# A long convolution with nine block products of a head in place of ten, and the summed index innermost

## The reference, cut to what matters

```python
vr = v.reshape(B, H, num_heads, L)                            # num_heads = 8; x1 and x2 are both the context
kv = vr[:, :, :, None, :] * x2r[:, :, None, :, :]             # b h i j l
y = irfft(rfft(kv, n=2 * L) * rfft(k, n=2 * L))[..., :L]      # causal convolution with the head's filter k[h]
y = y + kv * skip
out = jnp.einsum('bhijl,bhil->bhjl', y, x1r)                  # sum over i
```

## Time and profile before

| | |
|---|---|
| time, median of 3 runs | 2469.67 us (2468.76 to 2469.99) |
| profiled execution, its own time | 2451.03 us |
| span in its profile | 2448.9 us |
| PE busy in the span | 2185.6 us (89%) |
| DVE busy | 1212.2 us (49%) |
| ACT busy | 498.1 us (20%) |
| POOL busy | 437.4 us (18%) |

### The profile page before, as it was taken

The page is one execution under the profiler, slowest core; times in us unless marked ns, Lnnn a source line. Parts: engine busy times, 40 slices in busy tenths (PEclk is TensorE's granted clock), DMA queues, the critical chain, the costliest instruction groups (busy, mean ns, idle before and its releaser), DMA issues. The chain is left out here.

```text
span 2448.9 us, 30812 instructions
## 1 busy us (share of the span) xinstructions
PE 2185.6 (89%) x12383; PEld 1265.5 (52%) x12383; DVE 1212.2 (49%) x1811; ACT 498.1 (20%) x751; POOL 437.4 (18%) x445
## 2 busy tenths in 40 slices
PE   5888888867999989989999669899999999997964
PEld 3344444323444466645555346566665666664643
DVE  1456566655777752012222143445756666655354
ACT  1444444440000021111111011222222222121111
POOL 1111111113444413211111121101010110101000
PEclk9999999988999999999999879999999999998977
DMA  7000000004111047722211230101010110000000
GB/s 251 1 1 26 27 27 18 27 9 172 30 30 30 26 151 195 131 95 63 62 61 61 99 130 27 44 1 44 1 52 1 53 35 1 26 1 9 10 1 18
DMA packets 63856, 125.26 MB, mean 51 GB/s; under 512 B 12877, under 2 KB 13972, under 8 KB 63732
## 3 DMA queue, kind: packets, MB, share of 16 engines
q1 hardware_dynamic: 37492, 61.56, 7.6%
q10 hardware_dynamic: 19536, 43.26, 6.3%
q0 software_dynamic: 6704, 18.64, 2.7%
HBM read 92.18 MB, written 39.70 MB: 54 GB/s over the span
## 5 line engine op out<-in xcount | busy, mean ns | idle before, releaser
L863 PE MATMUL convB_conv<-kv,toep 128*128 128x512 f32 x640 | 277.8, 597 | 9.9 <-POOL kv L849 9.9
L1910 DVE RECIPROCAL tail_inv<-tail_ring 128x256 f32<-128x256 f32 x64 | 112.3, 1755 | 211.9 <-PE tail_ring L1566 211.9
L863 PEld LDWEIGHTS convB_conv<-kv,toep 128*128 128x128 f32 x640 | 122.6, 192 | 165.1 <-issue 156.6
L1294 PE MATMUL moe_gu_ps<-gu,moe_xT 128*128 x624 | 192.6, 462 | 2.2 <-DVE moe_xT L1357 2.2
L1294 PEld LDWEIGHTS moe_gu_ps<-gu,moe_xT 128*128 128x128 f32 x624 | 118.9, 191 | 79.3 <-issue 21.9
L849 POOL TENSOR_TENSOR kv<-vT,cT 128x512 f32 (+1 forms) x128 | 132.8, 1069 | 147.3 <-PE convB_conv L863 133.4
L888 DVE TENSOR_REDUCE vT<-prod 128x512 f32 (+1 forms) x128 | 138.2, 1080 | 16.7
L1741 POOL TENSOR_SCALAR_AFFINE_SELECT tail_expT<-tail_expT 128x1024 f32<-128x1024 f32 x64 | 70.9, 1107 | 368.8 <-ACT tail_expT L1803 368.7
L1312 PE MATMUL moe_y_ps<-down,moe_hT 128*128 (+1 forms) x234 | 110.7, 609 | 12.5 <-ACT moe_hT L1346 12.5
L1896 DVE TENSOR_TENSOR tail_allowed<-tail_scores,const_mask_bf 128x1024 f32<-128x1024 f32 x64 | 78.0, 1219 | 88.5 <-PE tail_scores L1518 87.9
L1735 POOL TENSOR_TENSOR tail_rstd_x<-tail_rstd_x,const_minus_half 128x2 f32<-128x2 f32 x32 | 22.3, 697 | 533.8 <-DVE tail_rstd_x L1868 533.8
(11 more groups left out here) (311 smaller groups left out, 3844.7 us busy)
## 6 DMA issues: line engine op xcount, KB each, us to landing
y_slots<-moe_y ACTq DMA_DIRECT2D x39, 256.0 KB, 2.0
toeplitz<-filt_pad SPq DMA_DIRECT2D x1, 8192.0 KB, 31.8
toep<-toeplitz SPq DMA_DIRECT2D x32, 256.0 KB, 2.6
gu<-in_L_ffn_gate_up_proj ACTq DMA_DIRECT2D x2, 2816.0 KB, 14.9
gu<-in_L_ffn_gate_up_proj SPq DMA_DIRECT2D x2, 2816.0 KB, 18.5
front_e<-in_ctx SPq DMA_DIRECT2D x8, 512.0 KB, 4.2
x_after<-x SPq DMA_DIRECT2D x8, 512.0 KB, 5.1
down<-in_L_ffn_down_proj ACTq DMA_DIRECT2D x2, 2048.0 KB, 18.3
```

The source lines that it names most:

```text
L863: ins = pe.matmul(conv[:, NC * p + lc, :], toep[p][:, lo:lo + P], kv[p][:, c].rearrange("p b i j -> p (b i j)"), start=c == 0, stop=c == lc)
L1294: ins = pe.matmul(gu_ps[:, s % 2, h, 0:HID], xT[:, c, :], wgu[c][:, e, h * HID:(h + 1) * HID], start=c == 0, stop=c == NC - 1)
L1910: link.after(dve.reciprocal(inv[c % 2][:], bank[:, S:2 * S]))
```

## The change

```diff
@@ front_stage, SP @@
                 load_x(0)
+                sp.dma_start(filt, filters).then_inc(filt_loaded, 16)
...
-                first_traffic(sp)
+                sp.wait_ge(steps_made, 2)
+                first_traffic(sp, filt, fall, rise)
...
+                        key = ("T", B - 2, len(T_UNITS) - 1)
+                        sp.wait_ge(quads.filled_sem(key), quads.count(key))
                         next_traffic(sp)
@@ front_stage, POOL @@
+                pool.wait_ge(filt_loaded, 16)
+                pool.tensor_tensor(fall, filt[:, 0:3 * P], filt[:, P:4 * P], ALU.subtract).then_inc(steps_made, 1)
+                pool.tensor_tensor(rise, filt[:, P:4 * P], filt[:, 0:3 * P], ALU.subtract).then_inc(steps_made, 1)
@@ front_stage, DVE @@
                 def combine(b, ab, t):
+                    if b + ab + t == 0:
+                        dve.wait_ge(pad_stored, 64)
@@ long_conv_stage @@
+        PARTS = {0: ((T0, 0),), 1: ((T1, 0), (T0, 1)), "both": ((T2, K01),), 2: ((T0, 2), (FALL, 1)),
+                 3: ((T1, 2), (RISE, 0), (T0, 3))}
+        KV_ORDER = (0, 1, K01, 2, 3)
...
+            @block.tensor
+            def _(pe):
+                for h in range(H):
+                    p = h % 2
+                    pe.wait_ge(mid.toep_loaded[p], 16 * (h // 2) + 16)
+                    for part in PARTS:
+                        last = max(KV_ORDER.index(c) for _, c in PARTS[part])
+                        pe.wait_ge(kv_ready, 5 * h + last + 1)
+                        bank = ring.claim(pe, (h, part))
+                        for n, (mat, c) in enumerate(PARTS[part]):
+                            ins = pe.matmul(bank, toep[p][:, mat * P:(mat + 1) * P], kv[p][:, c].rearrange("p b j i -> p (b j i)"),
+                                            start=n == 0, stop=n == len(PARTS[part]) - 1)
+                        ins.then_inc(ring.filled_sem((h, part)), 1)
...
+                for h in range(H):
+                    p = h % 2
+                    if h >= 2:
+                        pool.wait_ge(ring.filled_sem((h - 2, 3)), ring.count((h - 2, 3)))
+                    for n, c in enumerate(KV_ORDER):
+                        if c == K01:
+                            pool.wait_ge(kv_ready, 5 * h + n)
+                            pool.tensor_tensor(kv[p][:, K01], kv[p][:, 0], kv[p][:, 1], ALU.add).then_inc(kv_ready, 1)
+                        else:
+                            pool.tensor_tensor(kv[p][:, c], tokens_of(c, h), context_of(c, h, 3), ALU.mult).then_inc(kv_ready, 1)
...
+                for h in range(H):
+                    key = (h, "both")
+                    act.wait_ge(ring.filled_sem(key), ring.count(key))
+                    if h >= 2:
+                        act.wait_ge(ring.drained_sem((h - 2, 3)), ring.count((h - 2, 3)))
+                    act.copy(both[h % 2][:].rearrange("p b j i -> p (b j i)"), ring.tile(key)).then_inc(ring.drained_sem(key), 1)
...
+                def sums(h, lc):
+                    dve.tensor_reduce(vT[:, lc, :, h * NI:(h + 1) * NI], prod[lc % 2][:], AX_X, ALU.add)
+
+                for h in range(H):
                     for lc in range(NC):
-                        dve.wait_ge(conv_ready, NC * h + lc + 1)
-                        bank = conv[:, NC * p + lc, :].rearrange("p (b i j) -> p b i j", i=NI, j=NI)
-                        dve.tensor_tensor(prod[:, lc % 2], bank, over(context_of(lc, h), "i"),
-                                          ALU.mult).then_inc(prod_ready, 1)
-                        dve.wait_ge(prod_ready, NC * h + lc + 1)
-                        dve.tensor_reduce(vT[:, lc, :, bass.ds(h * NI, NI)],
-                                          prod[:, lc % 2].rearrange("p b i j -> p b j i"), AX_X, ALU.add)
+                        key = (h, lc)
+                        dve.wait_ge(ring.filled_sem(key), ring.count(key))
+                        bank = pairs(ring.tile(key))
+                        if lc < 2:
+                            dve.tensor_tensor(prod[lc][:], bank, context_of(lc, h, 2), ALU.mult).then_inc(ring.drained_sem(key), 1)
+                            dve.wait_ge(ring.drained_sem(key), ring.count(key))
+                        else:
+                            if lc == 2:
+                                dve.wait_ge(ring.drained_sem((h, "both")), ring.count((h, "both")))
+                            dve.tensor_tensor(total[lc - 2][:], bank, both[h % 2][:], ALU.add).then_inc(ring.drained_sem(key), 1)
+                            dve.wait_ge(ring.drained_sem(key), ring.count(key))
+                            link.after(dve.tensor_tensor(prod[lc - 2][:], total[lc - 2][:], context_of(lc, h, 2), ALU.mult))
+                        sums(h, lc)
@@ expand_filters @@
+    sp.dma_start(rows[:, 0:P], zeros).then_inc(pad_stored, 16)
+    sp.dma_start(rows[:, P:4 * P], filt[:, 0:3 * P]).then_inc(pad_stored, 16)
+    sp.dma_start(rows[:, 4 * P:6 * P], fall[:, 0:2 * P]).then_inc(pad_stored, 16)
+    sp.dma_start(rows[:, 6 * P:8 * P], rise[:, P:3 * P]).then_inc(pad_stored, 16)
+    sp.wait_ge(pad_stored, 64)
+    for at, lo, n in ((P, 0, 3 * P), (5 * P, 3 * P, P), (7 * P, 4 * P, P)):
+        up = bass.AP(tensor=rows.tensor, offset=rows.offset + at, ap=[[8 * P, H], [-1, P], [1, n]])
+        sp.dma_start(toeplitz[:, :, lo:lo + n], up).then_inc(toep_stored, 16)
```

More of the change, by code:

```diff
@@ L184, in project_rows, with front_stage @@
     return ins
-def front_stage(nc, consts, x_in, ctx_in, base_out, vT, cT, w, norm_w, skip, spare, first_traffic, next_traffic):
+def front_stage(nc, consts, x_in, ctx_in, base_out, vT, cT, w, norm_w, skip, spare, filters, pad_stored, first_traffic, next_traffic):
     HD = 16
@@ L811, in long_conv_stage @@
     with ExitStack() as ctx:
-        st = Stage(nc, ctx, "convB")
-        kv = [region.at(f"kv{p}", AT_PLAIN + p * 2 * KB4, [P, NC, B, NI, NI]) for p in range(2)]
-        prod = region.at("prod", AT_PLAIN + 4 * KB4, [P, 2, B, NI, NI])
+        st = Stage(nc, ctx, "conv")
+        kv = [region.at(f"kv{p}", AT_PLAIN + p * 5 * 4 * D, [P, NC + 1, B, NI, NI]) for p in range(2)]
+        prod = [region.at(f"prod{p}", AT_PLAIN + (10 + p) * 4 * D, [P, B, NI, NI]) for p in range(2)]
+        both = [region.at(f"both{p}", AT_SMALL + p * 4 * D, [P, B, NI, NI]) for p in range(2)]
@@ L815, in long_conv_stage @@
+        total = [region.at(f"total{p}", AT_SMALL + (2 + p) * 4 * D, [P, B, NI, NI]) for p in range(2)]
         conv = st.ps("conv", [P, 8, 512])
+        ring = Banks(st, "conv", [conv[:, k, :] for k in range(8)])
         kv_ready = st.sem("kv_ready")
[L817 to L821, removed]
-        def tokens_of(c, h):
-            return vT[:, c, :, bass.ds(h * NI, NI)]
@@ L826, in context_of @@
[L826 to L834, removed]
-        with nc.Block() as block:
+        linked = st.sem("linked")
+        T0, T1, T2, FALL, RISE = range(5)
+        K01 = NC
+        PARTS = {0: ((T0, 0),), 1: ((T1, 0), (T0, 1)), "both": ((T2, K01),), 2: ((T0, 2), (FALL, 1)),
+                 3: ((T1, 2), (RISE, 0), (T0, 3))}
@@ new lines, in long_conv_stage, with context_of, pairs @@
+        KV_ORDER = (0, 1, K01, 2, 3)
+        def tokens_of(c, h):
+            return vT[:, c, :, h * NI:(h + 1) * NI].unsqueeze(2).to_broadcast([P, B, NI, NI])
+        def context_of(c, h, axis):
+            return cT[:, :, c, h * NI:(h + 1) * NI].unsqueeze(axis).to_broadcast([P, B, NI, NI])
+        def pairs(tile):
+            return tile.rearrange("p (b j i) -> p b j i", i=NI, j=NI)
+        with nc.Block() as block:
+            @block.tensor
[11 more added lines that the diff above has]
+                        ins.then_inc(ring.filled_sem((h, part)), 1)
@@ L839, in _ @@
                 for h in range(2, H):
-                    sp.wait_ge(conv_ready, NC * h - NC)
+                    sp.wait_ge(ring.filled_sem((h - 2, 3)), ring.count((h - 2, 3)))
                     sp.dma_start(toep[h % 2][:], toeplitz[h]).then_inc(mid.toep_loaded[h % 2], 16)
@@ L2070, in decoder_kernel @@
         cT = region.at("cT", AT_CT, [P, B, NC, S])
-        toep = [region.at(f"toep{p}", AT_X2T + p * 4 * D, [P, D]) for p in range(2)]
+        toep = [region.at(f"toep{p}", AT_X2T + p * 20 * P, [P, 5 * P]) for p in range(2)]
         early = {k: region.at(f"early_{k}", n * 4 * NC * D, [P, NC, D]) for n, k in enumerate(("wq", "wk"))}
@@ L2080, in first_filters @@
             def first_filters(sp):
-                sp.wait_ge(toep_stored, 16)
+                sp.wait_ge(toep_stored, 48)
                 for h in range(2):
```

26 lines of the change are left out of this document (12 added, 14 removed).

## The result

The changed kernel takes **2440.4 us** (median of 4 runs, 2438.7 to 2441.3) where before took 2469.8 in the same session: ratio 0.987, 95% interval 0.9858 to 0.9882. The forecast was 2444.1. The direction was right, but 29.4 us are gone where I had 25.6. By the ratio, 0.987 of the 2469.67 that I started from is 2437.6, just under my range of 2438 to 2460; the quotient of the two medians is 0.988 and would give 2440.3, just inside it.

A forecast was written before the change was run, and what follows sets the result against it. PE was taken to bound the convolution stage and stay the bound; -27.5 + 1.2 (semaphores) + 0.5 (start) + 0.2 (end) = -25.6 us, taken off the runs' median, gave 2444.1 us, range 2438 to 2460.

The forecast's parts named there:

- PE's part: Convolution stage: nine products in place of ten over 32 heads, 7.72 us a head, 27.5 us less.
- The end: Convolution's end: from PE's last matmul to the last reduction's end 2.2 us in place of 2.0, so + 0.2.
- DVE's part: Convolution stage: DVE's steps sum to 6.66 us a head against PE's 7.72, with reductions at 0.68; the part that decides.
- The contention: Convolution: DVE products with two SBUF inputs wait for POOL, losing 0.35 and 0.3 us; DVE 7.3 us a head.
- Beside other work: ACT's copy, larger filter loads (6.9 us at most, under 7.72) and the longer filter expansion cost nothing.
- my doubled price of 80: Filter expansion to 640 columns: 40 us in place of 31.8, or 80 if its short pieces double it.
- The start: Front stage: the filter load issued ahead of wk and wv delays PE's first projection by 0.5 us.
- The 18.6 us: Median of the runs above the profiled execution's 2451.0 us; unplaced, so the gain was taken off the median.
- 1: Convolution: DVE takes over in part, its dependent steps at 0.82 us, 7.97 us a head; 2452 us, chance 0.14.
- 2: Convolution: both DVE products blocked in full by POOL, 8.5 us a head; 2469 us, no change, chance 0.07.
- 3: Convolution: the reduction over i gets no cheaper, DVE needs 8.9 us a head; 2482 us, slower, chance 0.07.
- 4: Gain not seen: a later load was the limit, or the front stage shifts by over 5 us; chance 0.04.

The follow-up runs named there:

- step_of_eight: The changed kernel with the columns back in the old order b, i, j, so the sum reads with a step of 8 numbers: 2469.7 us against before's 2451.4, ratio 1.0072.
- these six profiles: Profiles without gaps of the changed kernel, unchanged or with only its scatters delayed, limited or mostly left out; middle stage 183.0 or 183.1 us.
- before_b: The kernel before, unchanged, run against itself on the chip with gaps: 2471.5 us, ratio 0.9998.
- before_depth4: The kernel before with at most four scatters in flight, on a chip without gaps: 2453.8 us, ratio 1.0009.
- ten_innermost: The kernel before, ten products and its loop, with columns ordered b, j, i so the sum reads neighbours: 2450.4 us against 2451.4, ratio 0.9993.

## Why the prediction was right, and where it was not

- **PE's part** (27.5 us): right. A head takes 7.724 us against 7.72. From front barrier to convolution barrier the stage went from 281.7 to 255.5 us, 26.2 less; my terms for it (-27.5, + 1.1 for 15 semaphores, + 0.2 at the end) give -26.2. The end: last matmul at 831.1 + 0.59, last reduction until 833.9, 2.2 us, as I had it.
- **DVE's part**: right, and it decides, as step_of_eight shows: with the old order DVE is the bound. The reduction takes 686 ns (I had 0.68), dependent steps follow in 0.71 to 0.73. (One reading was off: the 1.7 us that DVE had to spare before take the written-out head's 0.71 a step; with the loop's 0.82 of the earlier trace rows it is 1.3. Nothing in the sum hangs on it.) DVE's and POOL's timelines in the kernel after:

```profile
700.41 0.69 DVE L917 TENSOR_TENSOR total<-conv_conv,both 128x512 f32<-128x512 f32 x1 [0.43 <-PE conv_conv L861]
701.14 0.93 DVE L919 TENSOR_TENSOR prod<-total,cT 128x512 f32<-128x512 f32 x1
702.11 0.69 DVE L904 TENSOR_REDUCE vT<-prod 128x64 f32<-128x512 f32 x1
...
706.29 0.69 DVE L919 TENSOR_TENSOR prod<-total,cT 128x512 f32<-128x512 f32 x1
```

```profile
700.46 2.54 POOL L882 TENSOR_TENSOR kv<-vT,cT 128x512 f32<-128x512 f32 x2 [1.79 <-PE conv_conv L861]
703.07 1.27 POOL L880 TENSOR_TENSOR kv<-kv 128x512 f32<-128x512 f32 x1
704.30 2.09 POOL L882 TENSOR_TENSOR kv<-vT,cT 128x512 f32<-128x512 f32 x2
```

- **The contention**: the mechanism holds, the size was too high. The product of part 3, at 701.14, stands behind POOL's kv0 and takes 0.93 in place of 0.69, and kv0 and kv1 together take 2.54 in place of 2.09: 0.24 us lost on DVE and 0.45 on POOL. The product of part 2 starts at 706.29, when POOL's last is all but over (706.39), and loses nothing. I had 0.35 + 0.3. As the Trainium skill has it (SBUF — State Buffer, "Who interferes with whom"), DVE stood until POOL's instruction was over; by the rows (kv0 of some 1.07 us ends at 701.53, the product at 702.07) it then took 0.54 us, not its whole 0.69.
- **Beside other work**: right. Filters land in 2.8 us, 6.4 at most. The expansion's copies, the last of which SP begins to issue at 71.7 us, took up to 88.4 us to land, beyond my doubled price of 80, and were down at least 250 us ahead of the first filter load at 462.0. ACT's first copy ends at 590.0.
- **The start**: too high. PE's first projection begins at 23.88 us in place of 23.79: 0.1, not 0.5. The 0.4 us off are less than the front stage's own spread in the unchanged kernel (579.1 us in one profile, 583.6 in before_b).
- **The step that failed** is the sum, "-27.5 + 1.2 + 0.5 + 0.2 = -25.6 us": it has no term for the stages behind the convolution, which puts them at nothing, and it gives no reason for that. The range had the same hole: its lower side was built from the convolution's starting matmuls and the median's own spread. The runs showed 27.2 us without gaps and 29.3 to 29.9 with them, while the convolution stage itself gave 26.2, as summed.
- **What stood in its place, without gaps**: the middle stage runs the same instructions in 183.0 us in place of 185.7, 2.7 less, at a granted clock of 0.99 in place of 0.97. From its end to the barrier ahead of the tail there are 350.8 or 350.9 us in these six profiles in place of 350.0 to 350.2 (351.9 in before_depth4), some 0.8 more. With the 26.2 that is 28.1; the measured 27.2 lies within what the front stage (from 574.0 to 581.0 us to its end) and the tail (1049.3 to 1053.4) move from one profile to the next.
- **With the gaps** 3.1 to 3.7 us of the gain lie outside the convolution, and where stays open. The middle stage doesn't tell: 204.3 us in before_b, and 201.4, 202.0 and 205.4 in three profiles of the changed kernel. In the three profiles of ten products on that chip the front stage ends at 579.1 to 580.5 us and the tail takes 1053.0 to 1053.4; in three of the changed kernel it is 575.2 to 576.9, and 1050.2 to 1052.4. Both stages spread as much without gaps.
- **The 18.6 us** that I could not place are the gaps among the scatters and the lower clock with them (204.3 against 185.7 us in before's middle stage): the profile was of the kind without gaps, the median of the kind with them, by their times. To take the gain off the median was sound, though I had no ground to know it: both kernels have the gaps alike. For the kind without gaps I had 2425.4, and the changed kernel's median is 2423.9.
- **Rivals**: 1 and 2 (DVE as the bound) didn't come. 3 was refuted for this kernel, whose reduction takes 686 ns, and its price is borne out by step_of_eight. Of 4, the front stage moved by less than its own spread.

## What to carry to other kernels

Fewer products on the bound engine pay in full only if the engine behind it has room for what is added; here the order of the columns made that room (+18 us without it, -27 us with it), and neither half shows its worth alone. When a profile and the timed runs differ by more than their spread, compare stage by stage with a second profile, of both kernels, before you take a gain from one off the other. Stages that a change doesn't touch are not worth nothing: here the middle stage moved by 2.7 us with the same instructions, a tenth of the gain, and the range should have had room for it. And look at several profiles before you give such a shift a cause: the tail moves by as much between two profiles of one kernel.

## What the runs showed of the hardware

- 32 scatters of 128 numbers of 4 bytes by POOL go with gaps in PE's work on one of the five chips that the experiments met, and not on the other four. They begin 24 to 27 us after the first scatter and make the middle stage some 18 us longer (204.3 in place of 185.7), in part by a lower granted clock (0.93 in place of 0.97). With 2 scatters they are gone.
- A DVE sum over runs of 8 costs 1.08 us for 128 x 512 with a step of 32 bytes and 0.686 with neighbours, output unchanged (ten_innermost against before, step_of_eight against the changed kernel).
- A DVE product with two SBUF operands and a POOL product slow each other: 0.93 for 0.69 and 2.54 for 2.09; when DVE had no idle time, 1055 ns in the mean and up to 1549.
- A semaphore that POOL clears at a stage's end costs 0.075 us, used or not (24 more: 3.0 us in place of 1.2).
- The middle stage took 183.0 us at a granted clock of 0.99 when PE had stood idle 4.01 us ahead of it, 185.7 at 0.97 behind 2.81 us, and 186.3 at 0.96 behind 5.71 us. Six profiles stand behind the first figure, and one behind the last.
